# A convolution and FFN block on one core: for the first two images, the ring of input chunks goes from two places to four and the ring of band matrices from three to six, the bands are written out in sixteen pieces instead of four, and each quarter of them is waited for by itself

## The chip, the cores and the metric

The kernel runs on one core of a Trainium2 chip. The metric is the device time of one execution in microseconds; lower is better. Before the change it is 3422.01 us, the median of three runs (3416.06 to 3424.34).

## The reference

The input is x, 32 images of 112 rows, 112 columns and 96 channels, float32. Two residual layers follow each other:

```python
x = x + conv_ref(_ln_c(x), conv_kernel)      # conv_ref(v) = depthwise 3x3 convolution of v, plus v
t = tokens(x)                                # 112*112 tokens of 96 channels per image
t = t + ffn_ref(_ln_t(t), W1, b1, W2, b2)    # 96 -> 384 -> 96, relu between
```

Both norms are over the 96 channels of one pixel. In the FFN the operands are rounded to an 8-bit float (5 exponent bits, 2 mantissa bits) and the results to a 16-bit one.

## The kernel before

**Data.** An image stands in SBUF with its 112 rows on the partitions. Work is cut into chunks of 8 columns (CW): 14 chunks are an image, 28 chunks are two images (UNIT), and the whole input is 448 chunks. A chunk is 112 partitions of 3072 bytes, 336 KB. The tensor `images` holds two buffers of two images each: one is filled by the normalisation while the other is convolved and read.

**The convolution** runs on TensorE along the rows: for each pair of channels (a group g; there are 48) and each of the three column offsets, a 112x112 banded matrix is multiplied with the normalised rows of two images. A pair of channels takes 12 matmul instructions in the profile's count. The banded matrices are not stored in the input. They are **built** in the head of the program (L319 on TensorE, L429 on ScalarE, L580 on VectorE): 112 set-ups, each four small matmuls into one of seven PSUM banks; the set-ups with an even number are copied out by VectorE, those with an odd number by ScalarE, into a stage of two slots that lies in the second buffer of `images`. A quarter (28 set-ups, 12 groups, 3528 KB) is complete when its last copy is done; `send` (L438) then writes it to the tensor `bands` in DRAM with one DMA on ScalarE's queue. From there the bands are loaded again and again (L281, 294 KB for a group) into `band_ring`, which has three places, once for each pair of images.

**The steps.** Every engine runs the same program of steps, c = -59, -58, ... Step c normalises chunk c + 57 (ScalarE columns 0 to 5 of the eight, L476; VectorE columns 6 and 7, L652), takes the statistics of chunk c + 58 (VectorE `bn_stats`, L602; then ScalarE's square root, L500), and SyncE issues the load of chunk c + 59 into `xn` (L274). VectorE begins its step by inverting the root (L630) and negating the mean (L634), on which ScalarE's normalisation waits. From c = -29 the convolution of the first two images runs, 96/28 channels in a step, beside the normalisation of the next two. From c = -3 on, the FFN joins, and after that the program is in its steady state. I call step c + 58 "step s" below: step s normalises chunk s - 1, and steps 0 to 22 also hold five set-ups each (two in step 22).

**Queues.** SyncE issues nearly all loads, in order, and each is behind a wait:

```python
def load_xn(r, n):
    for s in normed:
        wait(sp, s, LOOP * r + n - NORM_RING + 1)
...
def load_bands(r, c, t):
...
            wait(sp, conv_mm, 2 * GROUPS * r + n - BAND_RING + 1)
```

`normed` counts chunks that are normalised, so chunk n is loaded when chunk n - 2 is done with. In a step SyncE first issues `load_xn` and then `load_bands` for two steps later (L296), so that the bands stand in the queue behind the wait for the normalisation. Ahead of the first band load it waits for all four sends (L293). `xf` is the ring of the FFN, seven places of a chunk each; before the FFN starts it holds constants and weights of the set-up.

## Time and profile before

| | |
|---|---|
| time, median of 3 | 3422.01 us (3416.06 to 3424.34) |
| time of the profiled execution | 3413.97 us |
| its span | 3412.2 us |
| busy share of the span | DVE 94%, ACT 92%, PE 88%, POOL 56% |
| DMA | 714.47 MB, mean 209 GB/s |
| chain of work that ended last | DVE 62%, issue 14%, ACT 10%, PE 8%, DMA 4% |

The span is the time from the first to the last instruction in the profiled execution. PE is TensorE, DVE VectorE, ACT ScalarE, POOL GpSimd, SP SyncE; a name with q is the engine's queue, that is an instruction that issues a DMA. The shares are means over stages with different limits: the head of the program, until the FFN joins at about 290 us, is the only stage that the change touches.

### The profile page before, as it was taken

To read this page: it belongs to the slowest core of one execution; us is meant where nothing else is said; L and a number is where in the kernel's file an instruction comes from. 1 tells how busy PE (TensorE), PEld (TensorE's weight loads), DVE (VectorE), ACT (ScalarE), POOL (GpSimd) and SP (SyncE) were. 2 spreads that over 40 slices of the span, in tenths; PEclk is the share of its full clock that TensorE was granted. 3 is DMA by queue.
4 is the path that set the end of the run, shared out by engine and by line. 5 is a ranking of instruction groups with operands and counts; after the bars stand their busy time and mean duration, and the time that the engine had idled before them with its cause. 6 is when DMAs were issued, how large, how long until landed. Compare 5 with 4: busy or idle time off the path is not lost.

```text
span 3412.2 us, 87581 instructions
## 1 busy us (share of the span) xinstructions
PE 3017.2 (88%) x24902; PEld 2505.6 (73%) x24902; DVE 3207.9 (94%) x11739; ACT 3155.9 (92%) x7100; POOL 1921.0 (56%) x915
## 2 busy tenths in 40 slices
PE   3299999999999899989999999989999999999976
PEld 3287777777777777777777777777777777778744
DVE  5447999999999999999999999999999999999998
ACT  5578999999999999999999999999999999987776
POOL 0003666656666566656666566665666666666676
PEclk9999999999999999999999999999999999999966
DMA  4567777777777777777777777777777777766533
GB/s 146 160 195 210 229 227 222 223 213 225 223 228 222 205 224 227 224 207 231 222 225 224 213 224 227 224 219 219 222 221 229 226 222 223 228 200 183 162 119 101
DMA packets 277335, 714.47 MB, mean 209 GB/s; under 512 B 34809, under 2 KB 34914, under 8 KB 276834
## 3 DMA queue, kind: packets, MB, share of 16 engines
q1 hardware_dynamic: 271394, 694.12, 69.5%
q10 hardware_dynamic: 5440, 14.45, 1.3%
q8 instruction: 219, 3.59, 0.4%
q14 instruction: 282, 2.31, 0.2%
HBM read 539.84 MB, written 168.59 MB: 208 GB/s over the span
## 4 chain that ended last, share of the span: by engine, by line
DVE 62%; issue 14%; ACT 10%; PE 8%; DMA 4%; DVEq 1%; SPq 0%; ACTq 0%; POOL 0%; POOLq 0%
DVE stats L602 21%; DVE xq L639 18%; DVE hid L592 9%; PE conv_ps L387 5%; ACT images L476 5%; DVE images L652 4%; DVE hid L597 4%; ACT hid L455 3%; DMA xn<-in_x 2%; DVE xt_ps L626 2%; PE hid_ps L350 1%; DVE rstd L630 1%; DMA band_ring<-bands 1%; DVE neg_mean L634 1%; PE y_ps L365 1%
## 5 line engine op out<-in xcount | busy, mean ns | idle before, releaser
L387 PE MATMUL conv_ps<-images,band_ring 112*112 112x222 f32 (+1 forms) x9216 | 1941.0, 356 | 49.5 <-DMA band_ring<-bands 48.9
L387 PEld LDWEIGHTS conv_ps<-images,band_ring 112*112 112x112 f32 x9216 | 1605.6, 178 | 205.5 <-issue 47.2
L236 POOL TENSOR_TENSOR xf<-xf,y 112x768 f32<-112x768 f32 x448 | 951.8, 2124 | 1169.0 <-DVE y L619 1169.0
L455 ACT ACTIVATE hid<-hid_ps 128x896 f16<-128x896 f32 x1344 | 1190.7, 926 | 90.1 <-PE hid_ps L350 87.4
L231 POOL TENSOR_TENSOR xf<-xf,images 112x768 f32<-112x768 f32 x448 | 981.3, 2190 | 318.2 <-DMA xf<-in_x 302.8
L476 ACT ACTIVATE images<-xn,neg_mean,rstd 112x96 f32<-112x96 f32 x2688 | 1082.2, 555 | 28.8 <-DVE neg_mean L634 19.3
L365 PEld LDWEIGHTS y_ps<-w2t,hid 128*128 128x128 f16 x10752 | 575.7, 100 | 408.5 <-ACT hid L455 217.2
L365 PE MATMUL y_ps<-w2t,hid 128*128 128x96 f16 x10752 | 672.3, 210 | 207.5 <-ACT hid L455 182.5
L639 DVE SCALAR_TENSOR_TENSOR xq<-xf,stats,xt_ps 112x96 fp8e5<-112x96 f32 x3584 | 850.1, 332 | 0.0
L350 PE MATMUL hid_ps<-xt,w1t 96*128 96x448 fp8e5 x2688 | 683.1, 363 | 23.6 <-ACT xt L447 23.6
L592 DVE TENSOR_SCALAR hid<-hid,b1q 128x896 f16<-128x896 f16 x1344 | 609.3, 489 | 16.0 <-ACT hid L455 14.9
L602 DVE BATCH_NORM_STATS2 stats<-xn 112x6 f32<-112x192 f32 x1792 | 521.5, 370 | 100.6 <-DMA xn<-in_x 91.9
L602 DVE BATCH_NORM_STATS2 stats<-xf 112x6 f32<-112x192 f32 x1792 | 505.6, 361 | 0.0
L463 ACT ACTIVATE y<-y_ps 112x384 f16<-112x384 f32 x896 | 442.9, 494 | 20.2 <-issue 11.3
L487 ACT ACTIVATE images<-conv_ps 112x448 f32<-112x448 f32 x768 | 404.3, 544 | 10.8 <-PE conv_ps L387 10.6
L597 DVE TENSOR_SCALAR hid<-hid 128x2688 uint16<-128x2688 int16 x448 | 392.2, 875 | 0.0
L350 PEld LDWEIGHTS hid_ps<-xt,w1t 96*128 96x128 f16 x2688 | 240.5, 100 | 162.2 <-ACT xt L447 29.7
L652 DVE TENSOR_SCALAR images<-xn,stats,rstd 112x96 f32<-112x96 f32 x896 | 282.4, 390 | 0.0
L619 DVE TENSOR_TENSOR y<-y,b2q 112x768 f16<-112x768 f16 x448 | 257.1, 574 | 8.0 <-ACT y L463 5.1
L447 ACT ACTIVATE xt<-xt_ps 128x448 uint16<-128x448 uint16 x448 | 246.5, 550 | 7.0 <-PE xt_ps L333 7.0
L333 PE MATMUL xt_ps<-ident,xq 112*128 112x112 bf16 x1792 | 168.3, 218 | 27.0 <-issue 17.3
L500 ACT ACTIVATE std<-stats,eps 112x8 f32<-112x8 f32 x448 | 138.7, 310 | 50.8 <-DVE stats L602 50.3
(51 smaller groups left out, 692.8 us busy)
## 6 DMA issues: line engine op xcount, KB each, us to landing
band_ring<-bands SPq DMA_DIRECT2D x768, 294.0 KB, 5.1
xn<-in_x SPq DMA_DIRECT2D x448, 336.0 KB, 3.4
xf<-in_x SPq DMA_DIRECT2D x448, 336.0 KB, 5.0
out<-xf SPq DMA_DIRECT2D x448, 336.0 KB, 3.8
bands<-images ACTq DMA_DIRECT2D x4, 3528.0 KB, 15.1
xf<-in_L_ffn_W SPq DMA_DIRECT2D x2, 144.0 KB, 2.9
xf<-in_L_conv_kernel SPq DMA_DIRECT2D x3, 3.4 KB
xf<-in_L_ffn_b SPq DMA_DIRECT2D x1, 42.0 KB, 3.0
```

Of the source, the lines that this page charges most:

```text
L231: pool.tensor_tensor(x2, x2, images[:, b, i, :, cols].rearrange("p c w -> p w c"), ALU.add).then_inc(with_conv, 1)
L236: pool.tensor_tensor(res, res, y[:, e % 2], ALU.add).then_inc(summed, CW)
L350: mm = pe.matmul(hid_ps[:, k, u, 0:HALF * H], w1t[:, P * j:P * j + P], xt_8[0:C, e % 2, HALF // 2 * u:HALF // 2 * (u + 1)], start=True, st ...
L365: mm = pe.matmul(y_ps[:, C * w:C * w + C], hid[:, e % 2, TOK * j + tok:TOK * j + tok + P], w2t[:, j, :], start=(j == 0), stop=(j == J - 1))
L387: mm = pe.matmul(dst[:, :, lo:hi], band_ring[:, n % BAND_RING, PAIR * dx + i, :], images[:, m % 2, :, ch, lo + dx - 1:hi + dx - 1], start= ...
L455: nc.scalar.activation(hid[:, e % 2, TOK * j:TOK * (j + 1)].rearrange("p (u n) -> p u n", u=2), hid_ps[:, k, :, 0:HALF * H], ACT.Identity) ...
L463: nc.scalar.activation(y[:, e % 2, HALF * u:HALF * u + HALF, :], y_ps[0:H, 0:HALF * C].rearrange("p (w c) -> p w c", c=C), ACT.Identity).t ...
L476: op = nc.scalar.activation(images[:, b, i, :, cols.start + w], xn[:, n % NORM_RING, w, :], ACT.Identity, bias=neg_mean[:, n % 2, w:w + 1] ...
L592: dve.tensor_scalar(part_j, part_j, b1q[:, j:j + 1], None, ALU.add).then_inc(hid_biased, 1)
L597: dve.tensor_scalar(bits.bitcast(U16), bits.bitcast(I16), ROUND8, -ROUND8, ALU.add, ALU.add).then_inc(hid_quant, 1)
L602: op = dve.bn_stats(stats[:, e % 2, i, w:w + 2, :].rearrange("p w s -> p (w s)"), src[:, w:w + 2, :].rearrange("p w c -> p c w"))
L639: op = dve.scalar_tensor_tensor(out=xq_8[:, e % 2, w // 2, 0:C, w % 2], in0=xf[0:H, e % FFN_RING, w, :], scalar=stats[:, e % 2, 0, w, 1:2] ...
```

## The change

Four things are edited, all of them for the first two images only (chunks 0 to 27 and the groups of the first convolution).

1. Chunks 0 to 27 use a ring of four places: the two of `xn`, and places 5 and 6 of `xf`. Chunk n is loaded when chunk n - 4 is normalised. From chunk 28 on, the ring has its two places again.
2. The bands of the first two images use a ring of six: the three of `band_ring`, and places 1 to 3 of `xf`. SyncE waits in three later steps for the last groups of this convolution before the FFN's chunks go to those places. The constant matrix `taps_16` moves to place 0 of `xf`.
3. A quarter of the bands is sent in four pieces of three groups (882 KB each, a quarter of the 3528 KB), one in a step, in four steps that follow each other. A quarter counts as written at 64 instead of 16. SyncE waits for quarter q ahead of its first group, and the normalisation into the buffer that held the stage waits for quarters 0 and 2 at chunk 28 and for 1 and 3 at chunk 42.
4. ScalarE normalises five columns of chunks 0 to 27 and VectorE three (six and two before).

```diff
+FIRST_NORM_RING = 4
+FIRST_BAND_RING = 6
+FIRST_ACT_COLS = 5
...
+        STAGED_AT = {UNIT: (0, 2), UNIT + CHUNKS: (1, 3)}
...
+        def norm_place(n):
+            if n < UNIT:
+                k = n % FIRST_NORM_RING
+                return xn[:, k] if k < NORM_RING else xf[0:H, FFN_RING - FIRST_NORM_RING + k]
+            return xn[:, n % NORM_RING]
+
+        def act_cols(n):
+            return FIRST_ACT_COLS if n < UNIT else ACT_COLS
...
+        def norm_place_free(r, n):
+            return LOOP * r + n - (FIRST_NORM_RING if n < UNIT else NORM_RING) + 1
+
+        def band_place(first, n):
+            if first:
+                k = n % FIRST_BAND_RING
+                return band_ring[:, k] if k < BAND_RING else \
+                    xf[0:H, 1 + k - BAND_RING].rearrange("p w c -> p (w c)")[:, 0:TAPS * H] \
+                    .rearrange("p (n h) -> p n h", n=TAPS)
+            return band_ring[:, n % BAND_RING]
...
                 def load_xn(r, n):
                     for s in normed:
-                        wait(sp, s, LOOP * r + n - NORM_RING + 1)
-                    sp.dma_start(xn[:, n % NORM_RING], chunk_of(x, r, n)).then_inc(xn_in[n % NORM_RING], 16)
+                        wait(sp, s, norm_place_free(r, n))
+                    sp.dma_start(norm_place(n), chunk_of(x, r, n)).then_inc(norm_arrival(r, n)[0], 16)
...
-                            wait(sp, conv_mm, 2 * GROUPS * r + n - BAND_RING + 1)
-                            sp.dma_start(band_ring[:, n % BAND_RING], bands[ch // PAIR]) \
-                                .then_inc(band_in[n % BAND_RING], 16)
+                            first = t < CONV_AT + UNIT
+                            if first and n % QGROUPS == 0:
+                                sp.wait_ge(bands_out[n // QGROUPS], 16 * SENDS)
+                            ring = FIRST_BAND_RING if first or t == c and n < GROUPS + BAND_RING else BAND_RING
+                            wait(sp, conv_mm, 2 * GROUPS * r + n - ring + 1)
+                            sp.dma_start(band_place(first, n), bands[ch // PAIR]) \
+                                .then_inc(band_arrival(first, r, n)[0], 16)
...
                 def step(r, c, t):
+                    if t == c and 1 <= t + 3 <= FIRST_BAND_RING - BAND_RING:
+
+                        sp.wait_ge(conv_mm, GROUPS - FIRST_BAND_RING + BAND_RING + t + 3)
...
-                    if t + 2 == CONV_AT:
-                        for s in bands_out:
-                            sp.wait_ge(s, 16)
...
-                def send(q):
-
-                    for s in band_col:
-                        act.wait_ge(s, SETUPS // 2 * (q + 1))
-                    act.dma_start(bands[QGROUPS * q:QGROUPS * (q + 1)].rearrange("g h n k -> h g n k"),
-                                  band_stage[:, q % 2]).then_inc(bands_out[q], 16)
+                def send(q, k):
+
+
+                    if k == 0:
+                        for s in band_col:
+                            act.wait_ge(s, SETUPS // 2 * (q + 1))
+                    lo, hi = QGROUPS * k // SENDS, QGROUPS * (k + 1) // SENDS
+                    act.dma_start(bands[QGROUPS * q + lo:QGROUPS * q + hi].rearrange("g h n k -> h g n k"),
+                                  band_stage[:, q % 2, lo:hi]).then_inc(bands_out[q], 16)
...
-                        if n % SETUPS == SETUPS - 1:
-                            send(n // SETUPS)
+                    for q in range(QUARTERS):
+                        k = t - NORM_AT - (SETUPS * (q + 1) - 1) // STEP_SETUPS
+                        if c == t and 0 <= k < SENDS:
+                            send(q, k)
```

Place one is SyncE's queue where the head's first stage ends and the convolution starts (x12, x27 and the like count repeats; `xn<-in_x` is a chunk load, `band_ring<-bands` the load of one group). Before:

```order
L274 DMA xn<-in_x 112x768 x2
L274 DMA xn<-in_x 112x768 [waits normed_dve,normed_act] x27
L281 DMA band_ring<-bands 112x672 [waits bands_out2,bands_out3,bands_out1,bands_out0]
L281 DMA band_ring<-bands 112x672
L274 DMA xn<-in_x 112x768 [waits normed_dve,normed_act]
L281 DMA band_ring<-bands 112x672
L274 DMA xn<-in_x 112x768 [waits normed_dve,normed_act]
L281 DMA band_ring<-bands 112x672 [waits conv_mm] x2
```

Now, from the last chunks of the first two images on (those in `xf` are the ring's third and fourth place):

```order
L317 DMA xf<-in_x 112x768 [waits normed_dve,normed_act] x2
L317 DMA xn<-in_x 112x768 [waits normed_dve,normed_act]
L328 DMA band_ring<-bands 112x672 [waits bands_out0]
L328 DMA band_ring<-bands 112x672
L317 DMA xn<-in_x 112x768 [waits normed_dve,normed_act]
L328 DMA band_ring<-bands 112x672
L317 DMA xn<-in_x 112x768 [waits normed_dve,normed_act]
L328 DMA xf<-bands 112x672 x2
L317 DMA xn<-in_x 112x768 [waits normed_dve,normed_act]
L328 DMA xf<-bands 112x672
L328 DMA band_ring<-bands 112x672 [waits conv_mm]
```

The first band load waits for one quarter instead of four, and six groups can be asked for before one is used; the order of chunk loads and band loads in the queue is what it was: the first band load is still behind the load of chunk 28.

Place two is ScalarE's program around the first send (L434 and L481 are copies of set-ups, L476 and L526 the normalisation, L442 and L492 the send). Before:

```order
L476 ACTIVATE images<-xn,neg_mean,rstd 112x96 x6
L500 ACTIVATE std<-stats,eps 112x8
L434 ACTIVATE images<-hid_ps 112x72x4 x2
L442 DMA bands<-images 112x12x672
L434 ACTIVATE images<-conv_ps 112x72x4
L476 ACTIVATE images<-xn,neg_mean,rstd 112x96 x6
L500 ACTIVATE std<-stats,eps 112x8
L434 ACTIVATE images<-hid_ps 112x72x4 x2
L476 ACTIVATE images<-xn,neg_mean,rstd 112x96 x6
```

Now:

```order
L526 ACTIVATE images<-xf,neg_mean,rstd 112x96 x5
L550 ACTIVATE std<-stats,eps 112x8
L481 ACTIVATE images<-hid_ps 112x72x4 x2
L481 ACTIVATE images<-conv_ps 112x72x4
L492 DMA bands<-images 112x3x672
L526 ACTIVATE images<-xn,neg_mean,rstd 112x96 x5
L550 ACTIVATE std<-stats,eps 112x8
L481 ACTIVATE images<-hid_ps 112x72x4 x2
L492 DMA bands<-images 112x3x672
L526 ACTIVATE images<-xn,neg_mean,rstd 112x96 x5
```

Each send has moved behind the copies of its step and is a quarter as large; four steps hold one where one step did, always just ahead of the normalisation, and each normalisation has a column fewer.

## Rows read from the trace of the kernel before

**Rows 1.** The page: the span

```profile
span 3412.2 us, 87581 instructions
```

**Rows 2.** Windows by stage: busy of PE, PEld, DVE, ACT, POOL, then PEclk, DMA share, GB/s

```profile
0.00:162.70 162.70, 47.53 (x454) 44.04 (x454) 80.93 (x309) 89.01 (x249) 3.33 (x19) 1.00 0.48 151
162.70:291.80 129.10, 114.08 (x576) 103.59 (x576) 60.93 (x238) 95.88 (x252) 1.03 (x1) 0.99 0.71 198
```

**Rows 3.** Waits, 0 to 160 us: total us, times, longest us

```profile
DVE stats L602 <- DMA xn<-in_x: 54.8, 17, 8.1
```

**Rows 4.** The chain that ended last, 20 to 62 us: start, us, what

```profile
40.22 9.08 DMA xn<-in_x
```

**Rows 5.** Timeline: one step of the head without a wait for a load

```profile
27.06 2.33 ACT L476 ACTIVATE images<-xn,neg_mean,rstd 112x96 f32<-112x96 f32 x6
29.21 0.29 ACT L500 ACTIVATE std<-stats,eps 112x8 f32<-112x8 f32 x1
...
29.53 0.20 DVE L630 RECIPROCAL rstd<-std 112x8 f32<-112x8 f32 x1 [0.90 <-ACT std L500]
...
29.77 0.17 DVE L634 SCALAR_TENSOR_TENSOR neg_mean<-stats,rstd 112x8 f32<-112x8 f32 x1
29.86 0.60 DVE L652 TENSOR_SCALAR images<-xn,stats,rstd 112x96 f32<-112x96 f32 x2
29.98 2.33 ACT L476 ACTIVATE images<-xn,neg_mean,rstd 112x96 f32<-112x96 f32 x6
```

**Rows 6.** Timeline, 116 to 129 us: statistics, copies of set-ups, the next normalisation

```profile
116.45 1.15 DVE L602 BATCH_NORM_STATS2 stats<-xn 112x6 f32<-112x192 f32 x4 [0.23 <-DMA xn<-in_x]
117.52 0.44 DVE L585 COPY images<-hid_ps 112x288 f32<-112x288 f32 x1
117.87 0.45 DVE L585 COPY images<-conv_ps 112x288 f32<-112x288 f32 x1
...
126.39 0.43 DVE L585 COPY images<-y_ps 112x288 f32<-112x288 f32 x1
...
128.25 0.41 ACT L434 ACTIVATE images<-hid_ps 112x288 f32<-112x288 f32 x1 [0.34 <-PE hid_ps L325]
128.56 2.33 ACT L476 ACTIVATE images<-xn,neg_mean,rstd 112x96 f32<-112x96 f32 x6
```

**Rows 7.** Timeline: ScalarE's normalisation behind the third send

```profile
102.16 2.33 ACT L476 ACTIVATE images<-xn,neg_mean,rstd 112x96 f32<-112x96 f32 x6 [5.00 <-DVE images L585]
```

**Rows 8.** The tile xn, 0 to 160 us: normalisations (ns; first and last start, us), landing of loads

```profile
L476 ACT ACTIVATE images<-xn,neg_mean,rstd x157: 530/537/553, 17.9 to 159.9; 112x96 f32<-112x96 f32 x157
...
DMA to landing us min/median/max: 3.0/3.3/9.1
```

**Rows 9.** DMA issues, 0 to 160 us: size and median time to landing

```profile
bands<-images ACTq DMA_DIRECT2D x4, 3528.0 KB, 15.1
```

**Rows 10.** Windows: ten us within the first send, columns as in Rows 2

```profile
40.00:50.00 10.00, 0.00 (x0) 0.00 (x0) 1.48 (x7) 3.12 (x10) 0.00 (x0) 1.00 1.00 334
```

**Rows 11.** Timeline: from chunk 26's normalisation to the first convolution

```profile
159.87 2.33 ACT L476 ACTIVATE images<-xn,neg_mean,rstd 112x96 f32<-112x96 f32 x6 [0.47 <-DVE neg_mean L634]
...
162.72 0.78 SPq L281 DMA_DIRECT2D band_ring<-bands  x2
...
166.92 24.62 PE L387 MATMUL conv_ps<-images,band_ring 112*112 112x224 f32 x120 [37.95 <-DMA band_ring<-bands]
```

**Rows 12.** Waits of PE, 166 to 292 us: total us, times, longest us

```profile
PE conv_ps L387 <- DMA band_ring<-bands: 48.2, 10, 38.0
```

**Rows 13.** Timeline: the normalisation of chunks 28 and 55 on ScalarE

```profile
167.85 2.34 ACT L476 ACTIVATE images<-xn,neg_mean,rstd 112x96 f32<-112x96 f32 x6 [0.47 <-DVE neg_mean L634]
...
286.82 2.35 ACT L476 ACTIVATE images<-xn,neg_mean,rstd 112x96 f32<-112x96 f32 x6 [0.47 <-DVE neg_mean L634]
```

**Rows 14.** The chain that ended last: two groups of convolution at 206 us

```profile
206.25 6.43 PE conv_ps L387 x24
```

**Rows 15.** Windows: the stretch around it, columns as in Rows 2

```profile
200.00:220.00 20.00, 18.07 (x87) 16.39 (x87) 7.99 (x32) 14.37 (x40) 0.00 (x0) 0.91 0.63 176
```

More of the change, by code:

```diff
@@ L44, in metaformer @@
     assert 2 * UNIT % NORM_RING == 0 and 2 * UNIT % FFN_RING == 0
+    assert FIRST_NORM_RING % NORM_RING == 0 and GROUPS % FIRST_BAND_RING == 0
+    assert TAPS * H <= CW * C and 1 + FIRST_BAND_RING - BAND_RING <= FFN_RING - FIRST_NORM_RING + NORM_RING
     with ExitStack() as ctx:
@@ L100, in staged @@
             free[0] += n
-            assert free[0] <= FFN_RING * CW * C
+            assert free[0] <= (FFN_RING - FIRST_NORM_RING + NORM_RING) * CW * C
             return a
@@ L109, in metaformer @@
         is_centre = staged(KP, 1)
+        taps_16 = staged(KP, NB).bitcast(BF16)[:, 0:NB]
+        assert free[0] <= CW * C
         taps_in = staged(KP, NB)
@@ L123, in metaformer @@
         SETUPS = H // SETUP_COLS
+        SENDS = 4
         STEP_SETUPS = 5
@@ L135, in metaformer @@
         bands_out = [sem(f"bands_out{i}") for i in range(QUARTERS)]
-        xn_in = [sem(f"xn_in{i}") for i in range(NORM_RING)]
+        xn_in = [sem(f"xn_in{i}") for i in range(FIRST_NORM_RING)]
         xf_in = [sem(f"xf_in{i}") for i in range(FFN_RING)]
         x_out = [sem(f"x_out{i}") for i in range(FFN_RING)]
-        band_in = [sem(f"band_in{i}") for i in range(BAND_RING)]
+        band_in = [sem(f"band_in{i}") for i in range(FIRST_BAND_RING)]
         conv_mm, conv_saved, with_conv = sem("conv_mm"), sem("conv_saved"), sem("with_conv")
@@ L182, in dma_count, with norm_arrival, band_arrival @@
             return (per // ring) * 16 * r + 16 * (e // ring + 1)
+        def norm_place(n):
[5 more added lines that the diff above has]
+            return FIRST_ACT_COLS if n < UNIT else ACT_COLS
+        def norm_arrival(r, n):
+            if n < UNIT:
+                return xn_in[n % FIRST_NORM_RING], 16 * (n // FIRST_NORM_RING + 1)
+            k = n % NORM_RING
+            fewer = UNIT // NORM_RING - len(range(k, UNIT, FIRST_NORM_RING))
+            return xn_in[k], dma_count(r, n, NORM_RING) - 16 * fewer
+        def norm_place_free(r, n):
[7 more added lines that the diff above has]
+            return band_ring[:, n % BAND_RING]
+        def band_arrival(first, r, n):
+            if first:
+                return band_in[n % FIRST_BAND_RING], 16 * (n // FIRST_BAND_RING + 1)
+            fewer = GROUPS // BAND_RING - GROUPS // FIRST_BAND_RING
+            return band_in[n % BAND_RING], dma_count(r, n, BAND_RING, 2 * GROUPS) - 16 * fewer
         def setups(c, t):
@@ L471, in normalise @@
                         wait(act, with_conv, LOOP * r + n - LOOP + 1)
-                        if n == STAGED_FROM:
-                            for s in bands_out:
-                                act.wait_ge(s, 16)
+                        for q in STAGED_AT.get(n, ()):
+                            act.wait_ge(bands_out[q], 16 * SENDS)
+                    hi = min(hi, act_cols(n))
                     for w in range(lo, hi):
-                        op = nc.scalar.activation(images[:, b, i, :, cols.start + w], xn[:, n % NORM_RING, w, :],
+                        op = nc.scalar.activation(images[:, b, i, :, cols.start + w], norm_place(n)[:, w, :],
                                                   ACT.Identity, bias=neg_mean[:, n % 2, w:w + 1],
                                                   scale=rstd[:, n % 2, w:w + 1])
-                    if hi == ACT_COLS:
+                    if hi == act_cols(n):
                         op.then_inc(normed[0], 1)
@@ L613, in statistics_c @@
                         wait(dve, s, LOOP * r + n - 1)
-                    dve.wait_ge(xn_in[n % NORM_RING], dma_count(r, n, NORM_RING))
-                    moments(1, n, xn[:, n % NORM_RING]).then_inc(stats_c_done, 1)
+                    dve.wait_ge(*norm_arrival(r, n))
+                    moments(1, n, norm_place(n)).then_inc(stats_c_done, 1)
                 def add_y_bias(r, e):
@@ L647, in normalise @@
                     wait(dve, with_conv, LOOP * r + n - LOOP + 1)
-                    if n == STAGED_FROM:
-                        for s in bands_out:
-                            dve.wait_ge(s, 16)
-                    for w in range(ACT_COLS, CW):
-                        op = dve.tensor_scalar(images[:, b, i, :, cols.start + w], xn[:, n % NORM_RING, w, :],
+                    for q in STAGED_AT.get(n, ()):
+                        dve.wait_ge(bands_out[q], 16 * SENDS)
+                    for w in range(act_cols(n), CW):
+                        op = dve.tensor_scalar(images[:, b, i, :, cols.start + w], norm_place(n)[:, w, :],
                                                stats[:, n % 2, 1, w, 1:2], rstd[:, n % 2, w:w + 1],
```

14 lines of the change are left out of this document (6 added, 8 removed).

## The prediction

> **What bounds the kernel now.** I read the page first, then the windows by stage, because the change touches the head alone. Of the span of 3412.2 us [rows 1] the head takes 291.8 us, in two stages that look different [rows 2]. In the first, up to 162.7 us, no engine is near its limit: VectorE is busy for 80.9 us, ScalarE for 89.0, TensorE for 47.5, and the DMA share is 0.48. In the second, 129.1 us long, TensorE is busy for 114.1 us: that stage is nearly bound by the convolution. After that come 448 chunks in 3120.4 us, 6.97 us each, and no instruction of that loop is changed.
>
> So the question for the first stage is what it waits for. The list of waits says that VectorE's statistics stood 54.8 us waiting for a chunk, in 17 waits, the longest 8.1 us [rows 3]. The chain that ended last shows such a wait lying on the path, 9.08 us of load [rows 4]. The loads have two prices, 3.3 us in the median and 9.1 us at worst [rows 8]; the reader is to see what lies beside the long ones: a send of 3528 KB that needs 15.1 us to land [rows 9], during which the DMA engines are full, at 334 GB/s [rows 10]. With two places a load can only start when the chunk two before it is normalised, so that even the short landing is on the path. The normalisation of chunk 0 starts at 17.9 us and that of chunk 26 at 159.9 us [rows 8]: 142.0 us for 26 steps, 5.46 us a step.
>
> **What a step costs when no load is late.** One such step took 2.92 us from one normalisation on ScalarE to the next. Its parts are six columns in 2.15 us (27.06 to 29.21), root to reciprocal 0.32, reciprocal to negated mean 0.24, and from there to the normalisation 0.21 [rows 5]. With five columns ScalarE's part is 5/6 of 2.15, so 1.79 us, and the chain is 1.79 + 0.32 + 0.24 + 0.21 = 2.56 us. This is the step when no set-up is in it.
>
> With set-ups VectorE counts. From its reciprocal on it takes 0.24, then 0.09, then three columns at 0.24 (two are done in 0.60 [rows 5], and their end overlaps the next instruction), then the statistics, 1.07 until the first copy can start (116.45 to 117.52), and 0.36 for each copy [rows 6]. The first copy starts 0.24 + 0.09 + 0.72 + 1.07 = 2.12 us behind the reciprocal. In an even step VectorE has three copies: 2.12 + 1.08 = 3.20 us. In an odd step ScalarE has three, and the last of them waits for TensorE, which waits for VectorE's first copy of the step before to free a bank: from that copy to ScalarE's normalisation it is 2.17 us (126.39 to 128.56) [rows 6]. So the normalisation starts 2.12 + 2.17 = 4.29 us behind the reciprocal of the even step, 1.09 us behind its own, and the next reciprocal follows 1.79 + 0.32 later: 3.20 us again. Both kinds cost 3.2 us.
>
> **The change part by part.**
>
> *Ring of four for chunks.* A load is issued at the end of normalisation n - 4 and needed by the statistics of n, which start some 0.6 us behind the start of normalisation n - 1. That leaves 3 x 3.2 + 0.6 - 1.8 = 8.4 us in a step with set-ups and 6.5 us in one without, against 3.3 us alone. The waits go. Steps 2 to 21: 20 x 3.2 = 64.0 us. Step 22, with two set-ups: 2.7. Steps 23 to 27: 5 x 2.56 = 12.8. Together 79.5 us.
>
> *The sends' own waits stay.* The first piece of a quarter waits, as the whole did, for VectorE's last copy, and the normalisation is queued behind it on ScalarE; ScalarE was idle for 5.00 us ahead of one [rows 7], much of it because that copy was itself behind a late chunk. Without late chunks the copy ends 2.12 + 0.44 us behind the reciprocal (0.36 more where it is the second), the send costs about 0.35, and the normalisation starts at about 2.95, 3.3 and 2.95 us in the steps 5, 16 and 22 instead of 1.09, 0.45 and 0.45. That is 1.9 + 2.8 + 2.5 = 7.2 us; for the second quarter the last even set-up was in the step before, and there is no wait.
>
> *Twelve more issues.* Each stands on ScalarE ahead of the normalisation; one is about 0.35 us (estimated as a copy of a set-up and a little less, 0.44 us at most [rows 6]). In even steps VectorE's 3.20 covers them, in steps without set-ups ScalarE idles 0.47 us before the normalisation in any case [rows 11]. Five stand in odd steps: 1.8 us. If nothing covered them it would be 12 x 0.35 = 4.2.
>
> *Pieces instead of wholes.* A piece is 882 KB, 2.7 us at 334 GB/s, and holds a chunk's load back for at most about that, instead of the nearly 6 us of today (9.1 against 3.3) [rows 8]. But four steps in a row now ask for a piece and a chunk each, 1.25 MB, 3.7 us at 334 GB/s, where a step lasts 3.2. In four steps this runs up 2 us, which the 8.4 us of slack take (3.3 + 2.7 + 2). In the last quarter, the steps are 2.56 us, the backlog grows to about 4 us and the slack is 6.5: there I expect a wait. I take 3 us for all contention; the bounds are 0 and, if every send step becomes as long as its bytes, 12 x 0.5 + 4 x 1.1 = 10.4.
>
> The Trainium skill, page "DMA: Bandwidth & Descriptors", section "Queues, rings and completion order", has each DMA engine take turns between the queues at packet granularity. By that a chunk's load beside a send would land at about 4.3 us (its 1 us of bytes doubled), and pieces would be no better than wholes. The trace disagrees: 9.1 us [rows 8].
>
> *Bands.* The wait for a quarter instead of for all comes to nothing: SyncE reaches it behind the load of chunk 28, which waits for chunk 26, and the last piece (step 25) has landed by then, as the last whole had before. From the start of normalisation 26 to the first convolution it was 7.05 us [rows 11]; a column less makes it 6.7: 0.4 us won. If the last quarter's pieces landed late it would still not matter, since its first group is number 36.
>
> *The second stage.* Within it TensorE waited for bands 48.2 - 38.0 = 10.2 us, in nine waits (the longest, 38.0, is the end of the first stage) [rows 12]. Six places let SyncE ask early, so this cannot be more than 10.2 us of gain. But the band loads stay behind the chunk loads in the queue, and chunks here still have two places: chunks 28 to 55 went at (286.82 - 167.85) / 27 = 4.41 us each [rows 13], where the convolution needs 4.06 (48 groups, two of which take 4.74 us in undisturbed places, over 28 steps, the 4.74 is 24 of the 120 matmuls in 24.62 us, [rows 11], less that stretch's waits). A group that is asked for at the end of a normalisation is used two steps later, so TensorE will run at the pace of that loop, which I take at 4.23, between 4.06 and 4.41. That gives 28 x 0.18 = 5 us, from 0 to 10.
>
> **Sum.** First stage: 79.5 + 7.2 + 1.8 + 3.0 = 91.5 us instead of 142.0, so 50.5 us won; 0.4 at the start of the convolution; 5 in the second stage; loop and tail 0. Together 56 us, 1.6%. The profiled execution would go from 3413.97 to 3358 us. The median before, 3422.01, is 8 us above that execution, so the median after is put at 3422 - 56 = 3366 us.
>
> **Rivals.**
>
> *DMA bounds the first stage (0.20).* The 14.45 MB of sends (4 x 3528 KB) and 10 MB of chunks need 73 us at 334 GB/s, and 91.5 us is close to it. For it: the share is 1.00 whenever a send is under way [rows 10]. Against it: the mean share is 0.48 [rows 2]. If the send steps last as long as their bytes (10.4 instead of 3 us) and a wait of 4 us per quarter comes on top where landing exceeds the slack, the gain is 56 - 7 - 16 = 33 us: 3389 us.
>
> *Each transfer pays for itself (0.04).* If a piece did not overlap its neighbours and its end cost as much as a short load's beyond its bytes (3.3 - 1.0 = 2.3 us), a send step would be 3.7 + 2.3 = 6.0 us, 2.8 more than forecast, 45 us in sixteen: 3422 - 11 = 3411 us, at the edge of what can be told from no change. Rows 10 speak against it, since send and chunks together fill the engines. In a sentence of its own: the same page of the Trainium skill, section "Anatomy of one DMA — SWDGE (gpsimd) path", gives a fixed cost of about 2.0 us a transfer and a knee at 860 KB, so by it pieces of 882 KB would run at half efficiency if nothing overlapped them.
>
> *The second stage is freed too (0.11).* If the pace there falls to the convolution's, 10 us instead of 5 are won, and with no contention 3 more: 3422 - 64 = 3358 us.
>
> *Slower (0.03).* The loop after the head is taken as unchanged. It has a price that the head can't pay: at 206.25 us two groups took 6.43 us instead of 4.74 [rows 14], in a stretch where the granted clock was 0.91 [rows 15]. Were TensorE, now busy earlier and with fewer pauses, granted less later, each such pair costs up to 1.7 us; 33 more of them in 3120 us outweigh the gain, and twice as many would give 3478 us. Against it: the loop is VectorE's and ScalarE's, which have the highest busy shares of the span (94 and 92% in the table above), and TensorE has some slack in it.
>
> **How the numbers follow.** The forecast, 3366 us, has 0.62. Runs of before spread over 3416 to 3424, so 0.3% (10 us) is about what a measurement of this kernel can tell from no change. The range reaches from the case in which both stages are freed and the contention is nil, 3352 with the runs' own spread, to the DMA-bound case, 3390; that leaves out some 0.15. Its lower part: the copies' step of 3.2 us could be 3.0, 4 us less. Faster by over 0.3%: 0.62 + 0.20 + 0.11 and a little of what remains, 0.93. Within 0.3%: 0.04. Slower: 0.03.
>
> **What the profile after would show.** Waits of the statistics for a chunk in the first stage: a few us instead of 54.8, and those in the last quarter's sends. Normalisation 0 to 26 in 88 to 96 us, pairs of steps with set-ups in 6.4 us. The first convolution at about 116 us instead of 166.92. Landing of chunk loads 3.3 to 7 us, none at 9. Idle of ScalarE before three of the first pieces, 2 to 2.5 us each. In the second stage, chunks at about 4.2 us each and waits for bands near nothing. The end of the second stage near 236 us instead of 291.8, and the loop at 6.97 us a chunk. I am wrong if loads still end the waits in all four quarters (DMA-bound), if the step with set-ups is well off 3.2 us (the loop over TensorE's banks misread), if TensorE still waits 10 us for bands, or if the loop's pace moves.

## The result, and the profile after

The changed kernel takes 3365.57 us (median of 4 runs, 3359.27 to 3365.72) against 3419.74 us for the kernel before in the same comparison (3416.06 to 3424.34): ratio 0.9836, 95% interval 0.9819 to 0.9854. That is 54 us, or 1.6%, faster; the forecast was 3366 us and 56 us. (That the time itself is met within 1 us is luck: the kernel before came out 2.3 us lower in this comparison than the 3422.01 us from which the forecast was made.) A second comparison later, in five rounds, gave 0.9831 (0.9817 to 0.9844).

The total came out, but the parts did not: the first stage gave more than forecast, the second nothing. The windows by stage of the kernel after, with the same columns as [rows 2], cut at its first band load and at the end of the first convolution; the third is twelve microseconds within the first quarter's sends:

```profile
0.00:107.92 107.92, 47.54 (x454) 44.04 (x454) 86.31 (x339) 77.74 (x223) 3.33 (x19) 1.00 0.71 227
107.92:237.20 129.28, 114.90 (x576) 104.29 (x576) 59.33 (x232) 95.05 (x250) 0.04 (x1) 0.99 0.72 198
33.00:45.00 12.00, 6.31 (x64) 5.88 (x63) 9.36 (x36) 10.87 (x33) 0.00 (x0) 1.00 0.97 309
```

The first stage is 54.8 us shorter (162.7 to 107.9), with 5 us more of busy time on VectorE, which has a third column now, and 11 us less on ScalarE, whose sixth is gone. What has left the stage is the waiting for chunks, as the next list shows. The second is as long as it was, 129.3 us against 129.1.

VectorE's list of waits in the first 105 us of the kernel after:

```profile
DVE stats L654 <- DMA xn<-in_x: 1.1, 1, 1.1
DVE stats L654 <- DMA xf<-in_x: 0.2, 1, 0.2
```

Two waits for a chunk, 1.3 us, where [rows 3] had 54.8 us in 17. The DMA issues of the same stretch, as in [rows 9]:

```profile
bands<-images ACTq DMA_DIRECT2D x16, 882.0 KB, 8.0
xn<-in_x SPq DMA_DIRECT2D x14, 336.0 KB, 5.3
xf<-in_x SPq DMA_DIRECT2D x14, 336.0 KB, 6.0
```

The chunk loads land *later* in the median than before (5.3 and 6.0 us against the 3.3 of [rows 8]), because there is nearly always a piece beside them, but they are now asked for four chunks ahead and nobody waits.

ScalarE's normalisations (the first column of each chunk is the start) show the steps themselves. The timeline of the kernel after, a pair without and then a step with a piece, the third quarter's first send, and the last quarter:

```profile
39.47 1.98 ACT L526 ACTIVATE images<-xf,neg_mean,rstd 112x96 f32<-112x96 f32 x5
...
42.05 1.97 ACT L526 ACTIVATE images<-xf,neg_mean,rstd 112x96 f32<-112x96 f32 x5
...
45.87 1.97 ACT L526 ACTIVATE images<-xn,neg_mean,rstd 112x96 f32<-112x96 f32 x5
...
65.24 1.97 ACT L526 ACTIVATE images<-xf,neg_mean,rstd 112x96 f32<-112x96 f32 x5
...
70.65 0.90 ACT L526 ACTIVATE images<-xf,neg_mean,rstd 112x96 f32<-112x96 f32 x2 [2.74 <-DVE images L637]
...
73.52 1.97 ACT L526 ACTIVATE images<-xn,neg_mean,rstd 112x96 f32<-112x96 f32 x5
...
96.55 1.98 ACT L526 ACTIVATE images<-xf,neg_mean,rstd 112x96 f32<-112x96 f32 x5 [0.47 <-DVE neg_mean L686]
...
99.12 1.98 ACT L526 ACTIVATE images<-xn,neg_mean,rstd 112x96 f32<-112x96 f32 x5 [0.47 <-DVE neg_mean L686]
...
102.94 1.98 ACT L526 ACTIVATE images<-xn,neg_mean,rstd 112x96 f32<-112x96 f32 x5 [0.47 <-DVE neg_mean L686]
```

From 39.47 to 45.87 is 6.40 us for a pair with set-ups, 2.58 and 3.82; from 96.55 to 99.12 it is 2.57 us without. The step that ends at 70.65 is 5.41 us long (from 65.24) instead of 2.57, with ScalarE waiting for VectorE's last copy ahead of the send; the step behind it takes 2.87 instead of 3.82. The step that ends at 102.94 is 1.25 us too long: a chunk behind the last quarter's pieces, issued at 93.4 us and 7.4 us in landing.

The second stage is best read in the chain that ended last, of which these rows are one round:

```profile
134.28 0.32 SPq L317
134.64 4.46 DMA xf<-bands
139.24 4.75 PE conv_ps L434 x24
144.01 0.54 ACT images L537
144.56 0.20 ACT std L550
144.78 0.21 DVE rstd L682
145.22 2.35 ACT images L526 x6
147.59 0.32 SPq L317
147.96 4.53 DMA xf<-bands
```

The reader is to see that it closes on itself: SyncE issues a chunk load, which has waited for a normalisation, then the band load behind it; the band takes 4.5 us, two groups 4.75, ScalarE saves them, takes the root and normalises, and SyncE may go on. A round is 13.3 us (134.28 to 147.59) and three steps long, 4.44 us a step, where the convolution needs 4.06. TensorE's waits in this stage, 118 to 237 us, beside those of [rows 12]:

```profile
PE conv_ps L434 <- DMA xf<-bands: 8.8, 7, 1.8
```

Last, the first and last FFN result on GpSimd. Kernel after:

```profile
264.95 2.13 POOL L279 TENSOR_TENSOR xf<-xf,y 112x768 f32<-112x768 f32 x1 [3.87 <-DVE y L671]
...
3359.17 1.64 POOL L279 TENSOR_TENSOR xf<-xf,y 112x768 f32<-112x768 f32 x1 [2.69 <-DVE y L671]
```

Kernel before, the same two:

```profile
316.70 2.13 POOL L236 TENSOR_TENSOR xf<-xf,y 112x768 f32<-112x768 f32 x1 [3.23 <-DVE y L619]
...
3407.43 1.63 POOL L236 TENSOR_TENSOR xf<-xf,y 112x768 f32<-112x768 f32 x1 [2.69 <-DVE y L619]
```

The FFN starts 51.8 us earlier. In the profiled pair the last result is only 48.3 us earlier, since the loop, whose code is the same, took 3090.7 us before and 3094.2 after. That is noise of the loop: from the sixth result to the last, all fourteen profiles of this document lie between 3053.3 and 3059.5 us, and not in order of their heads. So I compare heads by their marks and kernels by their medians.

The marks have scatter too, since each comes from one execution, and a part of it is TensorE's clock. Here are the first convolution and the stretch from there to the first FFN result, columns as in [rows 2], in the kernel after and in one of the experiments below (e2):

```profile
112.69:236.15 123.46, 114.55 (x576) 104.26 (x576) 57.12 (x225) 92.41 (x243) 0.00 (x0) 0.99 0.71 196
236.15:264.95 28.80, 24.18 (x143) 20.07 (x142) 23.87 (x89) 21.71 (x54) 10.94 (x5) 0.94 0.77 212
...
119.06:239.70 120.64, 112.36 (x575) 102.65 (x576) 56.82 (x223) 92.21 (x243) 0.00 (x0) 1.00 0.70 199
239.70:267.00 27.30, 22.32 (x143) 19.02 (x142) 25.39 (x91) 21.56 (x54) 10.99 (x6) 1.00 0.84 233
```

The granted clock is 0.99 and 0.94 in the first, 1.00 in both stretches of the second. In the kernel after, a pair of groups that takes 4.75 us elsewhere took 6.43 on the chain, 1.7 us more, when a part of it ran at the lower of the clock's two levels, 1.2 instead of 2.4 GHz (0.73 of full speed in the mean over the pair):

```profile
182.85 6.43 PE conv_ps L434 x24
```

The kernel before had such a pair as well [rows 14], and 0.93 in the stretch behind the convolution, so that before and after compare fairly. But a second profile of the unchanged file of the kernel after (g1 below) had 1.00 over the whole convolution, and its 576 matmuls took 122.3 us instead of 123.5. Before a difference of 1 to 3 us behind 110 us is laid to an edit, the clock of both stretches has to be compared.

### The profile page after: what moved, and what is told of

Its sections match the earlier page's. It is cut to its first block, busy times and chain, and to the rows that moved or that the text cites. A ratio compares the mean times of both kernels' runs of the same rounds, so it can differ in the third digit from the quotient of the medians.

```text
span 3364.0 us, 87592 instructions
## 1 busy us (share of the span) xinstructions
PE 3014.8 (90%) x24902; PEld 2505.1 (74%) x24902; DVE 3211.1 (95%) x11767; ACT 3142.8 (93%) x7072; POOL 1921.2 (57%) x915
## 4 chain that ended last, share of the span: by engine, by line
DVE 66%; issue 14%; PE 9%; ACT 8%; DMA 2%; DVEq 1%; SPq 0%; ACTq 0%; POOL 0%; POOLq 0%
DVE stats L654 22%; DVE xq L691 19%; DVE hid L644 10%; PE conv_ps L434 6%; DVE hid L649 5%; DVE images L703 5%; ACT images L526 3%; ACT hid L505 3%; DVE xt_ps L678 2%; PE hid_ps L397 1%; DVE rstd L682 1%; DVE neg_mean L686 1%; DVEq L183 1%; PE y_ps L412 1%; DVE y L671 1%
## 5 line engine op out<-in xcount | busy, mean ns | idle before, releaser
L434 PE MATMUL conv_ps<-images,band_ring 112*112 112x222 f32 (+1 forms) x8928 | 1884.4, 356 | 29.8 <-DMA band_ring<-bands 29.5
L434 PEld LDWEIGHTS conv_ps<-images,band_ring 112*112 112x112 f32 x8928 | 1553.2, 178 | 180.5 <-issue 31.9
L526 ACT ACTIVATE images<-xn,neg_mean,rstd 112x96 f32<-112x96 f32 x2590 | 1044.5, 556 | 21.3 <-DVE neg_mean L686 16.8
L644 DVE TENSOR_SCALAR hid<-hid,b1q 128x896 f16<-128x896 f16 x1344 | 594.6, 473 | 16.4 <-ACT hid L505 15.3
L654 DVE BATCH_NORM_STATS2 stats<-xn 112x6 f32<-112x192 f32 x1736 | 498.7, 356 | 46.7 <-DMA xn<-in_x 42.5
L654 DVE BATCH_NORM_STATS2 stats<-xf 112x6 f32<-112x192 f32 x1848 | 515.1, 347 | 0.2 <-DMA xf<-in_x 0.2
L703 DVE TENSOR_SCALAR images<-xn,stats,rstd 112x96 f32<-112x96 f32 x882 | 270.8, 376 | 0.0
```

Of the source, the lines that this page charges most:

```text
L434: mm = pe.matmul(dst[:, :, lo:hi], band_place(t < CONV_AT + UNIT, n)[:, PAIR * dx + i, :], images[:, m % 2, :, ch, lo + dx - 1:hi + dx - 1 ...
L526: op = nc.scalar.activation(images[:, b, i, :, cols.start + w], norm_place(n)[:, w, :], ACT.Identity, bias=neg_mean[:, n % 2, w:w + 1], sc ...
L644: dve.tensor_scalar(part_j, part_j, b1q[:, j:j + 1], None, ALU.add).then_inc(hid_biased, 1)
L654: op = dve.bn_stats(stats[:, e % 2, i, w:w + 2, :].rearrange("p w s -> p (w s)"), src[:, w:w + 2, :].rearrange("p w c -> p c w"))
```

## The experiments

All kernels do the whole computation. The marks, from each one's timeline: the start of ScalarE's normalisation of chunk 0 to that of chunk 26; the start of the first convolution; from the first to the last start of the 576 matmuls of the first convolution; the first FFN result. Ratios are to the kernel before in the same comparison.

| kernel | chunks 0 to 26 | first conv. | 576 matmuls | first FFN result | median | ratio (95%) |
|---|---|---|---|---|---|---|
| before | 142.0 | 166.9 | 122.4 | 316.7 | | 1 |
| changed | 87.2 | 112.7 | 123.5 | 265.0 | 3365.6 | 0.9836 (0.9819 to 0.9854) |
| e1 two chunk places | 131.3 | 156.0 | 120.1 | 303.7 | 3400.7 | 0.9963 (0.9951 to 0.9976) |
| e2 whole sends | 93.9 | 119.1 | 120.7 | 267.0 | 3365.4 | 0.9860 (0.9844 to 0.9877) |
| e3 three band places | 87.5 | 113.0 | 123.7 | 265.8 | 3359.0 | 0.9836 (0.9819 to 0.9852) |
| e4 six columns | 90.7 | 115.4 | 121.3 | 266.2 | 3362.5 | 0.9848 (0.9831 to 0.9864) |
| f1 bands first | 87.3 | 113.2 | 115.6 | 256.2 | 3356.3 | 0.9824 (0.9807 to 0.9840) |
| f2 longer chunk ring | 87.1 | 110.6 | 115.0 | 254.6 | 3352.7 | 0.9812 (0.9795 to 0.9830) |
| f3 both | 87.0 | 111.2 | 111.4 | 255.1 | 3351.2 | 0.9802 (0.9785 to 0.9819) |
| f4 ring of four alone | 96.2 | 122.1 | 123.0 | 273.1 | 3372.2 | 0.9869 (0.9847 to 0.9891) |
| g1 changed, again | 87.2 | 112.4 | 122.3 | 264.3 | 3359.8 | 0.9831 (0.9817 to 0.9844) |
| g2 both, again | 87.5 | 110.8 | 112.2 | 251.9 | 3352.3 | 0.9807 (0.9794 to 0.9821) |
| g3 later sends | 84.6 | 109.6 | 121.0 | 258.0 | 3361.2 | 0.9837 (0.9823 to 0.9850) |
| g4 both, later sends | 87.0 | 110.3 | 112.6 | 250.6 | 3350.7 | 0.9806 (0.9793 to 0.9820) |

e1 to e4 were compared with one another and with the kernel before (3414.44 us), likewise f1 to f4 (3418.78) and g1 to g4 (3418.09). The first four each undo one part of the change. The theory was that the chunk ring and the pieces make the first stage, and that SyncE's order, not the band places, holds the second.

**e1, two places for chunks.**

```diff
-FIRST_NORM_RING = 4
+FIRST_NORM_RING = 2
```

> The changed kernel with the chunk ring of the first two images back at two places; pieces, six bands and five columns stay. My theory: the ring is the main term, because even a short landing of 3.3 us is on the path with two places. A pair of steps without a send took 9.0 us before; with a column less it is 8.6, 13 pairs are 112 us, and pieces in sixteen steps add 0.5 to 1 us each, so normalisation 0 to 26 takes 118 to 128 us instead of 87 and the time is 31 to 41 us above the changed kernel. Rival: the sends in one piece were the trouble, and pieces alone cure it: then it is at most 15 us above.

The ring is the main term, as the theory says; the stage is 131.3 us, 3 over my upper end. What the 3 us are was not tested. My sum had left out ScalarE's three waits for VectorE's last copies ahead of a send, which are 11.5 us together in e1's trace (7.2 in the kernel after), so that it need not be the pieces. VectorE's waits in its first 150 us:

```profile
DVE stats L654 <- DMA xn<-in_x: 42.4, 13, 6.2
```

Thirteen waits, one for each pair of chunks, the longest 6.2 instead of 8.1 us: with pieces (and a column fewer) the waits are shorter and still on the path. Undone alone, the ring costs 44 of the 54.8 us; the time is 1.3% above the changed kernel's.

**e2, whole sends.**

```diff
-        SENDS = 4
+        SENDS = 1
```

> The changed kernel with each quarter sent by one DMA, in the step where it was the first piece. My theory: loads stand behind most of a send of 15 us; the ring of four gives 8.4 us of slack against landings of 9 to 12 us, so each of the four sends costs a wait of 2 to 4 us, and 12 issues less give back 1 to 2: 5 to 14 us above the changed kernel, with waits of the statistics for a chunk at all four sends. Rival: four places cover a whole send too (or the queues take turns and nothing is held back), so that pieces are worth nothing: within 2 us.

The stage is 6.7 us longer, and ScalarE's wait for statistics behind late chunks says where, four waits for the four sends:

```profile
ACT std L550 <- DVE stats L654: 7.1, 4, 2.8
```

In the changed kernel the same wait is 1.1 us, once. So the rival, that four places cover a whole send, falls for the first stage. At the FFN's first result only 2.0 us of the 6.7 are left, but up to 3 us of that are the clock: as the windows above show, the kernel after had two stretches at the lower level on the way there and e2 none. The ratio, 0.9860 against 0.9836 (8 us), agrees in size with the 6.7 us; the two intervals overlap a little, so that the time alone does not prove the worth of the pieces.

**e3, three places for bands.**

```diff
-FIRST_BAND_RING = 6
+FIRST_BAND_RING = 3
```

> The changed kernel with the band ring of the first two images back at three places. The trace after the change shows the second stage no shorter than before (123.8 us for its 576 matmuls against 122.8), and its chain runs normalisation, SyncE, band load, two groups, their save, root, reciprocal, normalisation, 13.4 us for three steps. My theory: SyncE's order holds the bands back, not the number of places; three places cost at most 2 us in the second stage and the time is 0 to 2 us above the changed kernel. Rival: six places do help and something else took the gain away: 5 to 10 us above.

No difference: 123.7 us against 123.5, the same ratio, and TensorE's waits, 118 to 238 us, are those of six places:

```profile
PE conv_ps L434 <- DMA band_ring<-bands: 9.1, 8, 1.7
```

In this order of SyncE's queue six places are worth nothing. Whether they are worth something once the order is changed was not tried: all kernels below but f4 have six.

**e4, six columns on ScalarE.**

```diff
-FIRST_ACT_COLS = 5
+FIRST_ACT_COLS = 6
```

> The changed kernel with six columns on ScalarE for chunks 0 to 27. By the sums of the prediction a pair of steps with set-ups goes from 6.4 to 6.5 us (VectorE's first copy comes 0.24 earlier, ScalarE's column costs 0.36), a step without set-ups from 2.56 to 2.92: 10 x 0.12 + 5 x 0.36 = 3 us above the changed kernel. Rival: ScalarE bounds every step, 27 x 0.36 = 10 us; or VectorE does, and six columns are 27 x 0.24 = 6 us faster.

3.4 us in the first stage, where 3 were worked out, and the pair with set-ups in its timeline is 6.53 us, where 6.5 were:

```profile
39.03 2.34 ACT L526 ACTIVATE images<-xf,neg_mean,rstd 112x96 f32<-112x96 f32 x6
...
45.56 2.33 ACT L526 ACTIVATE images<-xn,neg_mean,rstd 112x96 f32<-112x96 f32 x6
```

Neither rival holds (10 us longer, 6 us shorter): no one engine bounds a step. The round through both engines and TensorE's banks, as the prediction worked it out, gives the measured numbers.

**f1, bands first.** In the steps of the first convolution, SyncE asks for bands before it waits for the normalisation.

```diff
                 def step(r, c, t):
+                    early = CONV_AT + 1 <= t + 2 < CONV_AT + UNIT
+                    if early:
+                        load_bands(r, c + 2, t + 2)
...
-                    load_bands(r, c + 2, t + 2)
+                    if not early:
+                        load_bands(r, c + 2, t + 2)
```

> The changed kernel with SyncE's order turned round during the first convolution: in a step the bands of two steps later are asked for ahead of the chunk load, so that they no longer stand behind the wait for the normalisation. My theory: that wait is what holds the second stage at 123.5 us; the 576 matmuls then take 115 to 119 us, the rest being the chunk loop over two places, waits for bands fall under 3 us, and the time is 4 to 8 us under the changed kernel. Rival: the second stage is held by the chunk loop (two places in xn) alone, and TensorE's waits for bands are only its echo: 122 us or more and no change in the time. Second rival: the DMA engines are too busy there, so bands asked for earlier land later: waits for bands stay above 6 us.

115.6 us instead of 123.5, and no wait for bands is left in TensorE's list, 118 to 231 us:

```profile
PE conv_ps L438 <- ACT images L541: 2.2, 4, 0.9
```

That settles it between the queue's order and its rivals: the same loads of the same bytes, only issued ahead of the wait. The DMA engines were not too busy, and the chunk loop over two places still allows 4.17 us a chunk. Since the clock was at 1.00 here, the fair number is the one against g1: 6.7 us. In the kernel's time the edit can't be told from the changed kernel (0.9824 and 0.9836, with intervals that overlap for the most part).

**f2, four places for chunks 0 to 47.**

```diff
+FIRST_CHUNKS = 48
...
-            if n < UNIT:
+            if n < FIRST_CHUNKS:
                 k = n % FIRST_NORM_RING
```

(and the same bound in the two functions beside it)

> The changed kernel with the ring of four places kept for chunks 0 to 47 instead of 0 to 27; SyncE's order as it is. A chunk load then waits for the chunk four before, so it and the bands behind it are asked for two steps earlier. My theory (SyncE's order) says the bands are freed as well: 576 matmuls in 114 to 117 us, first convolution 2 to 3 us earlier, since the first band load no longer waits for chunk 26: 8 to 12 us under the changed kernel. The rival of the chunk loop says the same of this kernel, so that it is the pair with the one before that tells them apart; the rival of busy DMA engines says 121 us or more.

115.0 us, the first convolution 2.1 us earlier than in the changed kernel: within the expectation. It frees the bands by another way, as the wait ahead of them is now for a chunk four back. It frees the chunks too: VectorE's waits for them are 12.8 us between 105 and 238 us, where the changed kernel has 40.6, so that this run by itself does not tell bands from chunks.

**f3, both.** 

> Both edits together: bands ahead of chunk loads in SyncE's queue, and four places for chunks 0 to 47. If four places already free the bands, the order has nothing left to give: within 2 us of the one with four places alone, second stage 114 to 117 us. If the order gives more, it is because chunk loads still hold bands up: 2 to 4 us less.

111.4 us; the second expectation, that chunk loads still held bands up a little, is the one met (3.6 us less than f2 in this stage, 2.8 by the second profile, g2). TensorE now runs 432 matmuls, three quarters of the convolution, in one piece on the chain that ended last:

```profile
111.18 83.41 PE conv_ps L439 x432
```

The FFN's first result, however, is no earlier than in f2 (255.1 and 254.6). The same kernel's second profile has it at 251.9; the granted clock from the end of the convolution to there was 0.89 in the first and 0.94 in the second.

**f4, the ring of four alone.**

```diff
+        SENDS = 1
+FIRST_BAND_RING = 3
+FIRST_ACT_COLS = 6
```

(lines of the changed kernel with other values; four places stay)

> Of the change only the ring of four for chunks 0 to 27: whole sends, three bands, six columns. With what the single parts measured (whole sends 93.9 - 87.2 = 6.7 us in the first stage, six columns 90.7 - 87.2 = 3.4, three bands 0.3), normalisation 0 to 26 should take 87.2 + 10.4 = 97.6 us if they add up, against 142.0 before the change, and the time be 6 to 10 us above the changed kernel: four fifths of the gain in one edit. Rival: with whole sends the columns don't matter, since loads are waited for anyway: 94 us.

96.2 us; the sum of the parts was 97.6, so they nearly add. One edit makes 45.8 of the 54.8 us of the first stage, and 46.6 us in the median (3418.78 to 3372.23). By the ratios it is 11 us above the changed kernel, 1 over my range.

**g1 to g4, in five rounds.**

> The changed kernel once more, in five rounds on the chip that also runs the next three, so that they can be compared with it. Ratio to before 0.983 to 0.985; 576 matmuls of the second stage in 122 to 124 us.

As expected, and the base for the other three.

> Bands ahead of chunk loads and four places for chunks 0 to 47, once more. The marks of the first profile put the FFN's first result 9.9 us ahead of the changed kernel's: 8 to 13 us under it in the median. If the clock's dips in the loop ate the gain, it would be under 4.

3352.27 against 3359.78 us: 7.5 us, just under the range, and no execution of the one lies among those of the other. The marks say 12.4 us at the first FFN result; the rest is within the loop's scatter.

```diff
-        SENDS = 4
+        SENDS = 3
...
-                        k = t - NORM_AT - (SETUPS * (q + 1) - 1) // STEP_SETUPS
+                        k = t - NORM_AT - (SETUPS * (q + 1) - 1) // STEP_SETUPS - 1
```

> The changed kernel with the first piece of a quarter one step later, when VectorE's last copy is long done, and three pieces of four groups instead of four of three, so that the last one leaves in the same step. It tests the term of the prediction for the sends' own waits: in the changed kernel the normalisation was held 1.9, 2.8 and 2.5 us in steps 5, 16 and 22, about 1 us of which the next step gave back. If the waits were on the path, normalisation 0 to 26 takes 81 to 83 us instead of 87.2. Rival: the pieces of 1176 KB hold loads and the stage up, what is won is lost to waits for chunks: 86 us or more.

Neither: 84.6 us, 2.7 of some 6 won in the first stage of this profile, and the median is not better. (The profiled execution was the fastest of five. That its first FFN result is 6.3 us ahead of g1's is in part the clock, 1.00 all the way there, while g1 has 0.94 behind the convolution.) The timeline of ScalarE shows what came in place of the wait for VectorE:

```profile
51.40 0.41 ACT L481 ACTIVATE images<-conv_ps 112x288 f32<-112x288 f32 x1 [2.63 <-DMA bands<-images]
```

The stage has two slots, and a set-up of the third quarter must wait until the first is written. ScalarE has two such waits, 4.6 us together, and VectorE one of 1.6; VectorE's waits for chunks are 1.6 us, hardly more than in the changed kernel. So of the two reasons in my rival, loads and the stage, it was the stage. In the changed kernel this wait is there already, 0.9 us once (a copy at 51.72 us), which the prediction did not have; it made that step 0.1 us longer.

> All three edits: later sends, bands ahead of chunk loads, four places for chunks 0 to 47. If the stages are independent the gains add: 12 to 18 us under the changed kernel, near 3350 us where it has 3365. Rival: the second stage starts earlier and meets the last quarter's pieces, whose landing delays bands or the chunks from 28 on, and 2 to 4 us are lost again.

3350.74 us, not to be told from g2: the later sends brought nothing. But 87.0 us in the first stage is no sign of the rival. Up to chunk 27 the instructions of g3 and g4 are the same, and the two part at the same wait for the stage, which lasted 2.63 us in g3 and 3.22 in g4, with two late chunks of 1.6 and 1.5 us beside it in g4 and one of 0.7 in g3. So one first stage gave 84.6 and 87.0 us, and the 2.7 us of g3 are not shown to be a gain. The kernel that I would keep is g2's: 0.9807 of the kernel before (0.9794 to 0.9821), 0.2% under the changed one.

## Why the prediction was right, and where its steps failed

**What bounds it.** Right. Waits for chunks in the first stage went from 54.8 to 1.3 us, and e1 shows that two places bring 42.4 of them back.

**The step without a late load.** Right to about a hundredth of a microsecond: the pair with set-ups 6.40 us, forecast 6.4; the step without 2.57, forecast 2.56; e4 confirms the model by its 6.53, forecast 6.5. (The single starts are 2.58 and 3.82 us apart, not 3.2 and 3.2, because the normalisation stands 0.45 us behind its reciprocal in one step and 1.09 in the next; only the pair is to be compared.)

**The sends' own waits.** The single waits were right: the three steps are 1.9 (27.30 to 33.01, where an odd step takes 3.82), 2.8 and 2.5 us too long, as forecast. Missed: in step 17 the set-ups were already there and 0.95 us came back. 7.2 was 6.3. And g3 and g4 show that the term can't simply be removed, since behind it stands the wait for the stage.

**Twelve more issues.** "Five stand in odd steps: 1.8 us" was mis-sized: an odd step with a piece takes 3.88 us (54.95 to 58.83) against 3.82 without. In the timeline the issue at 58.47 us runs beside the copy that starts at the same time. 0.3 us in all for the five.

**Contention.** "I take 3 us" was 1.3: the one late chunk in the last quarter's pieces, the place that was named. e2 puts the value of the pieces at 6.7 us in the stage. The DMA-bound rival falls: the engines were at 0.97 share and 309 GB/s in the first quarter's send steps, close to full, and still none of those steps waited for a chunk. The rival in which each transfer pays for itself falls with it: send steps without another wait took 3.88 us and, in the last quarter, 2.57, not 6.0. From the Trainium skill's taking turns by packets (page "DMA: Bandwidth & Descriptors", section "Queues, rings and completion order") the prediction had an estimate of 4.3 us for a chunk's load beside a send, with pieces no better than wholes. The runs disagree, as the trace before did: with whole sends (e2) a chunk's load lands at up to 9.5 us, with pieces at up to 7.5, and the pieces saved 6.7 us. How an engine orders its packets no run here shows.

The first stage was thus 87.2 us, not 91.5: 54.8 us won instead of 50.5. The first convolution then began 7.14 us behind the start of chunk 26's normalisation, not 6.7: the first bands took 4.6 us to land. And chunk 0 started 0.4 us later than before, which is scatter (17.8 to 18.8 us in the fourteen profiles).

**The second stage.** This is the step that failed. "Six places let SyncE ask early", and "TensorE will run at the pace of that loop, which I take at 4.23": the pace stayed at 4.41 us a chunk ((232.62 - 113.50) / 27), the same as in [rows 13]. I had named the band loads' place behind the chunk loads and then treated the chunk loop as a loop of its own, from which TensorE would take its pace. In the trace the two are one loop, through SyncE's queue, the band load, two groups and their save, and it has no slack to give. The waits for bands, which I had named as the sign of being wrong, were 8.8 us against 10.2 before. So 5 us were -1.1 (122.4 to 123.5 for the matmuls; 122.3 in g1, so nothing rather than a loss). f1 and f3 open that loop, and give 7.9 and 12.1 us, or 6.7 and 10.9 against g1 with the same clock. f1 alone moves nothing but the issue of the band loads, and so shows the place. Its 4.17 us a chunk is near my 4.23: the size of the chunk loop was right, and the belief that TensorE would follow it alone was wrong. The rival "the second stage is freed too" did not come with this change; f3 is what it takes.

Then the start of the FFN took back another 1.4 us (53.2 us ahead at the last matmul, 51.8 at the first result); what waits there was not tried, and from the last matmul of the convolution to that result the profiles whose clock was at 1.00 take 27.2 to 27.6 us, the others 27.4 to 32.5, so it may be no more than the clock. The errors, +4 in the first stage, -6 in the second and -2 in small terms, cancelled in part: 56 us forecast, 51.8 at the head's end, 54.2 in the medians. The total was nearer than its parts deserved.

**The wait for a quarter** came to nothing in this kernel, as forecast, but only just: the first band load is issued at 107.92 us, behind the load of chunk 28 at 107.56, and the last piece had landed at 107.15. In f2, where the first band load goes out at 101.32 us and the last piece lands at 107.85, one wait for all four quarters would have held it back by about 6.5 us (an estimate from these two times).

**The slower rival** did not come: the granted clock over the span is 0.974 against 0.975, and the loop's pace is the same within its scatter.

## What to carry to other kernels

A ring gets its value from what its loads wait for, not from its size: four places for chunks took 46 us off (f4), six for bands none (e3), because the bands' loads stood in an in-order queue behind another wait. Before deepening a ring, follow its load back through the issuing queue; putting the issue ahead of the foreign wait (f1) took about 7 us off a stage from which the places had taken nothing. And when a stage's parts are forecast one by one, check each mark in the trace after, for a right total can hide two wrong terms. For marks a few microseconds apart, look at the granted clock of both stretches and at a second profile of the same kernel before naming a cause.

## What the runs showed of the hardware that I had not expected

A piece of 882 KB takes 8.0 us to land in the median, 10.1 at most, though its bytes are 2.7 us at the 334 GB/s of [rows 10]: at one piece and one chunk a step the DMA engines are at a share of 0.97 (33 to 45 us), and within a quarter each piece is issued before the one ahead of it has landed. A DMA issue on ScalarE's queue, 0.31 us long, delayed the next activation by only 0.06 us where a copy was running ahead of it. And two profiles of one and the same kernel can have the lower clock in different places: over the first convolution the granted clock was 0.99 in the one and 1.00 in the other (g1).
